# Attention values on 64x64 array tiles, and a slot that opens with scores, then the probabilities' transposition, then projections

## The reference, cut to what matters

```python
def attn_layer(x, Wqkv, qs, ksc, Wo):
    q, k, v = jnp.split(x @ Wqkv, 3, -1)            # then split into 16 heads of 64
    q = l2norm(q) * qs
    k = l2norm(k) * ksc
    q = q * cos * scale + rotate_half(q) * sin * scale
    k = k * cos * inv + rotate_half(k) * sin * inv
    out = local_attention(q, k, v)
    return out @ Wo
...
def local_attention(q, k, v):                        # keys: the window before and the own one
    sim = jnp.einsum('bhwie,bhwje->bhwij', bq, bk2) * QK_SCALE
    sim = jnp.where(mask, -jnp.finfo(sim.dtype).max, sim)
    attn = jax.nn.softmax(sim, -1)
    out = jnp.einsum('bhwij,bhwje->bhwie', attn, bv2)
...
for i in range(DEPTH):
    x = attn_layer(shift_tokens(x), ...) + x
    x = ffn_layer(shift_tokens(x), ...) + x
```

## Time and profile before

| | us |
|---|---|
| median of 3 runs | 1662.98 |
| lowest, highest | 1661.52, 1663.18 |
| the profiled execution's own time | 1662.44 |
| its span, first to last instruction | 1660.6 |
| PE busy in it | 1581.1 |
| DVE busy | 1471.4 |
| ACT busy | 1430.6 |
| POOL busy | 1313.8 |

### The profile page before, as it was taken

One profiled execution on the slowest core, in us unless ns is written; L12 is line 12 of the kernel. 1 busy time (PEld: TensorE's weight loads), 2 busy tenths in 40 slices (PEclk: granted clock), 3 DMA queues, 4 the chain that ended last, 5 costly groups with the idle time before them and its releaser, 6 DMA issues.

```text
span 1660.6 us, 68799 instructions
## 1 busy us (share of the span) xinstructions
PE 1581.1 (95%) x25860; PEld 1210.2 (73%) x25860; DVE 1471.4 (89%) x3011; ACT 1430.6 (86%) x2851; POOL 1313.8 (79%) x1305
## 2 busy tenths in 40 slices
PE   7879999999999999999999999999999999999995
PEld 5657777777777777777777777777777777777773
DVE  4499999999999999999999999999999999999874
ACT  4267998998999899899889989989998999999985
POOL 6188888888888888888888888888888888778855
PEclk9799999999999999999999999999999999999997
DMA  4111111111111111111111111111111101110100
GB/s 138 51 39 40 41 34 38 32 46 37 46 38 32 38 38 43 44 40 33 32 38 44 46 42 32 33 32 51 40 43 38 32 28 41 40 33 27 32 22 26
DMA packets 41425, 66.39 MB, mean 40 GB/s; under 512 B 7072, under 2 KB 16032, under 8 KB 41376
## 3 DMA queue, kind: packets, MB, share of 16 engines
q1 hardware_dynamic: 40224, 65.38, 13.2%
q10 hardware_dynamic: 1152, 0.34, 0.1%
HBM read 20.61 MB, written 1.05 MB: 13 GB/s over the span
## 4 chain that ended last, share of the span: by engine, by line
PE 58%; DVE 26%; issue 12%; ACT 2%; DVEq 1%; DMA 0%; POOL 0%; ACTq 0%; POOLq 0%
PE ps_s L539 13%; PE ps_a L539 11%; PE ps_qk L539 10%; PE ps_f L539 8%; PE ps_po L539 7%; DVE qk_rot L1269 5%; PE ps_v L539 5%; DVE qk L1267 4%; PE ps_po L658 4%; DVE ssq L1275 4%; DVE row_sum L1311 3%; DVE row_max L1302 3%; DVE prob L1305 2%; PE ps_f L747 1%; DVE xc L1324 1%
## 5 line engine op out<-in xcount | busy, mean ns | idle before, releaser
L436 POOL TENSOR_TENSOR qk<-qk,rnorm 128x512 f32<-128x512 f32 x384 | 393.0, 1044 | 132.1 <-DVE rnorm L1295 123.3
L428 POOL TENSOR_TENSOR qk<-qk,qk_rot 128x512 f32<-128x512 f32 x384 | 484.4, 1283 | 0.0
L443 POOL TENSOR_TENSOR prob<-prob,row_inv 128x512 f32<-128x512 f32 x192 | 200.4, 1044 | 115.5 <-DVE row_inv L1314 115.5
L1275 DVE TENSOR_REDUCE ssq<-squares 128x8 f32<-128x512 f32 x384 | 260.4, 678 | 3.4 <-ACT squares L959 3.4
L1267 DVE TENSOR_TENSOR qk<-ps_qk,table 128x512 f32<-128x512 f32 x384 | 262.2, 683 | 1.1
L1269 DVE TENSOR_TENSOR qk_rot<-ps_qk,table 128x512 f32<-128x512 f32 x384 | 260.7, 679 | 0.0
L959 ACT ACTIVATE squares<-ps_qk 128x512 f32<-128x512 f32 x384 | 232.1, 604 | 11.5 <-PE ps_qk L539 3.8
L953 ACT COPY p_bd<-ps_po 64x512 f32<-64x512 f32 x378 | 217.1, 574 | 21.0 <-PE ps_po L658 18.7
L539 PEld LDWEIGHTS ps_s<-ident,qk 128*128 128x128 f32 x1528 | 170.9, 140 | 77.6 <-DVE prob L1305 64.1
L539 PE MATMUL ps_s<-ident,qk 128*128 128x128 f32 x1528 | 202.9, 276 | 23.8 <-DVE prob L1305 22.9
L539 PE MATMUL ps_qk<-w_hi,xs_hi 128*128 (+1 forms) x384 | 188.7, 491 | 12.9 <-DVE qk_rot L1269 6.8
(11 more groups left out here) (207 smaller groups left out, 3490.4 us busy)
## 6 DMA issues: line engine op xcount, KB each, us to landing
v_back<-v_own SPq DMA_DIRECT2D x192, 192.0 KB, 2.4
w_raw<-in_wqkv SPq DMA_DIRECT2D x48, 192.0 KB, 2.4
v_back<-v_own SPq DMA_DIRECT2D x96, 64.0 KB, 2.1
wo_sb<-in_wo SPq DMA_DIRECT2D x12, 256.0 KB, 3.0
w_sb<-in_w SPq DMA_DIRECT2D x6, 341.0 KB, 3.0
w_sb<-in_w SPq DMA_DIRECT2D x6, 192.0 KB, 2.5
x_in<-in_x SPq DMA_DIRECT2D x4, 256.0 KB, 4.7
out<-s_out SPq DMA_DIRECT2D x8, 128.0 KB, 1.9
```

The costliest lines, as they stand in the source:

```text
L428: nc.gpsimd.tensor_tensor(qk[:, s, i, :], qk[:, s, i, :], qk_rot[:, s, i, :], ALU.add).then_inc(added, 1)
L436: nc.gpsimd.tensor_tensor(heads(qk[:, s, i, :]), heads(qk[:, s, i, :]), rnorm[:, s, 8 * i:8 * i + 8].unsqueeze(2).to_broadcast([P, 8, HEAD ...
L443: nc.gpsimd.tensor_tensor(heads(prob[:, s, :]), heads(prob[:, s, :]), row_inv[:, s, :].unsqueeze(2).to_broadcast([P, 8, HEAD]), ALU.mult). ...
L1275: V.tensor_reduce(ssq[:, s, 8 * i:8 * i + 8], heads(squares[:, s, OCTET * i:OCTET * i + OCTET]), AX, ALU.add).then_inc(ssq_done, 1)
```

## The change

`values` gets tiles of 64 rows by 64 columns. The key positions' two halves (`later` = 0, 1; each is one window) are multiplied apart, each with its own 32 columns of probabilities, and the two row tiles write to two banks. So `p_bd` with its zeros becomes `p_t`, a plain copy of the transposition; `keep_p` is one copy of 128 rows where it was two of 64, and the memset of `p_bd` goes. The 16 matmuls of a unit become 32, which move 32 columns where they moved 64.

The two banks are `ps_po` and `ps_q`, of each the first 256 columns; four banks are now one tensor, `ps_vpqk`, whose name the order of the changed kernel shows for `ps_v`, `ps_po`, `ps_q` and `ps_k`. Since `values` writes to `ps_q`, it waits for `q_scaled` of unit u (`pe.wait_ge(q_scaled, u + 5)`, with its own u being four less), and the next q projection waits for `attn_copied`. The q projection moves behind `scores` and `turn_p`. No other engine's order is changed but for `keep_p`.

```diff
@@ values
-            def values(u, n, j, s, ps=ps_po):
+            def values(u, n, j, s):
+
+                pe.wait_ge(q_scaled, u + 5)
+                values_into(valued, u, n, j, s)
+
+            def values_into(area, u, n, j, s):
 
                 pe.wait_ge(p_turned, u + 1)
                 pe.wait_ge(v_shifted[j], (n + 1) * (32 if j % 2 else 16))
+                nc.tensor.sem_inc(pe_passed, 1)
                 for c in range(PAIRS):
                     for odd in range(2):
+                        v = v_own if odd else v_back
                         for head in range(2):
-                            v = v_own if odd else v_back
-                            o = ps[64 * head:64 * head + 64, P * c:P * c + P].rearrange(
-                                "p (h o q) -> p h o q", h=2, o=2)[:, :, odd, :]
-                            last = mm(o, v[:, j, 64 * (2 * c + head):64 * (2 * c + head) + 64],
-                                      p_bd[:, s, 8 * head + 4 * (c // 2) + 2 * odd + c % 2].rearrange("p a b -> p (a b)"), True, True,
-                                      skip_group_check=True)
+                            for later in range(2):
+                                rows = slice(64 * later, 64 * later + 64)
+                                to = 64 * c + WINDOW * odd
+                                at = P * (2 * head + c // 2) + 64 * odd + WINDOW * (c % 2)
+                                last = mm(area[64 * head:64 * head + 64, later, to:to + WINDOW],
+                                          v[rows, j, 64 * (2 * c + head):64 * (2 * c + head) + 64],
+                                          p_t[rows, s, at:at + WINDOW], True, True, skip_group_check=True)
@@ body of TensorE
-                    project(n, j, 0, ps_q, q_scaled, q_done)
                     if live(u - 3):
                         scores(u - 3, (j - 3) % UNITS, (j - 3) % 2)
                     if live(u - 4):
                         turn_p(u - 4, j % 2)
+                    if live(u - 5):
+                        wait(pe, attn_copied, u - 4)
+                    project(n, j, 0, ps_q, q_scaled, q_done)
                     project(n, j, 1, ps_k, k_scaled, k_done)
@@ ScalarE
-                for h in range(2):
-                    rows = slice(64 * h, 64 * h + 64)
-                    last = copy(p_bd[rows, s, :, h, :], ps[rows, :].rearrange("p (g q) -> p g q", q=WINDOW))
-                last.then_inc(p_turned, 1)
+                copy(p_t[:, s, :], ps[:]).then_inc(p_turned, 1)
...
-                copy(attn_t[:, PAIRS * octet:PAIRS * octet + PAIRS, 1 + P * tile:1 + P * tile + P],
-                     ps[:].rearrange("p (c t) -> p c t", t=P)).then_inc(attn_copied, 1)
+                copy(attn_t[:, PAIRS * octet:PAIRS * octet + PAIRS, 1 + P * tile:1 + P * tile + P].rearrange(
+                    "p c (g t) -> p g c t", g=2), area.rearrange("p g (c t) -> p g c t", t=64)).then_inc(attn_copied, 1)
```

More of the change, by code:

```diff
@@ L70, in bank, with banks @@
             return ctx.enter_context(nc.psum_tensor(name, [P, 512], F32))
-        def bank_pair(name):
-            return ctx.enter_context(nc.psum_tensor(name, [P, 2, 512], F32))
+        def banks(name, n):
+            return ctx.enter_context(nc.psum_tensor(name, [P, n, 512], F32))
         def sem(name):
@@ L112, in build @@
         prob = sb("prob", [P, 2, OCTET])
-        p_bd = sb("p_bd", [P, 2, PAIRS * 4, 2, WINDOW])
+        p_t = sb("p_t", [P, 2, OCTET])
         row_max = sb("row_max", [P, 2, 8])
@@ L149, in build @@
         w1_early = [staged[l % 2][:, 2 * FF * (l // 2):2 * FF * (l // 2 + 1)] for l in range(DEPTH)]
-        ps_qk, ps_s = bank_pair("ps_qk"), bank_pair("ps_s")
-        ps_q, ps_k, ps_qs, ps_tk = ps_qk[:, 0, :], ps_qk[:, 1, :], ps_s[:, 0, :], ps_s[:, 1, :]
-        ps_v, ps_po, ps_a, ps_f = (bank(n) for n in ("ps_v", "ps_po", "ps_a", "ps_f"))
+        ps_vpqk, ps_s = banks("ps_vpqk", 4), banks("ps_s", 2)
+        ps_v, ps_po, ps_q, ps_k = (ps_vpqk[:, i, :] for i in range(4))
+        ps_vp, ps_pq, ps_qk = (ps_vpqk[:, i:i + 2, :] for i in range(3))
+        ps_qs, ps_tk = (ps_s[:, i, :] for i in range(2))
+        ps_a, ps_f = (bank(n) for n in ("ps_a", "ps_f"))
         def scored(pair):
             return pair[:, :, 0:OCTET // 2]
+        valued = scored(ps_pq)
         x_loaded = [sem(f"x_loaded_{p}") for p in range(TWOS)]
@@ L381, in _ @@
         def _(pool):
-            nc.gpsimd.memset(p_bd[:], 0.0)
             nc.gpsimd.memset(k_t[:, :, :, 0:WINDOW], 0.0)
@@ L650, in turn_into, with turn_p @@
                 last.then_inc(done, 1)
-            def turn_p(u, s, ps=ps_po):
-                if ps is ps_po:
+            def turn_p(u, s, ps=ps_po, turning=True):
+                if turning:
                     wait(pe, attn_copied, u)
@@ L835, in drain @@
                 pe.wait_ge(q_scaled, END)
+                pe.wait_ge(attn_copied, a)
                 turn_into(ps_q, c, 0, 0)
@@ L844, in drain @@
                 scores(c, 2, 0, ps_qk, False)
-                values(a, LAST, 0, 0)
+                pe.wait_ge(v_copied, END)
+                values_into(scored(ps_vp), a, LAST, 0, 0)
                 ln_spread(LAST - 2, END, STEPS + BATCHES - 4)
-                pe.wait_ge(v_copied, END)
-                turn_p(b, 1, ps_v)
                 ln_mean(LAST - 1)
                 scores(d, 3, 1, ps_s, False)
+                pe.wait_ge(attn_copied, a + 1)
+                turn_p(b, 1, ps_v, False)
                 ff_up(LAST - 2, 0)
-                pe.wait_ge(attn_copied, a + 1)
-                values(b, LAST, 1, 1)
+                values_into(scored(ps_vp), b, LAST, 1, 1)
                 ln_variance(LAST - 1)
                 ff_up(LAST - 2, 1)
-                turn_p(c, 0, ps_v)
+                pe.wait_ge(attn_copied, b + 1)
+                turn_p(c, 0, ps_v, False)
                 ff_up(LAST - 2, 2)
                 pe.wait_ge(sub_done, c + 1)
-                values(c, LAST, 2, 0, ps_k)
+                values_into(scored(ps_qk), c, LAST, 2, 0)
                 out_projection(LAST, 0)
-                turn_p(d, 1, ps_v)
+                turn_p(d, 1, ps_v, False)
                 ln_spread(LAST - 1, END + 1)
                 pe.wait_ge(sub_done, END)
+                pe.wait_ge(attn_copied, c + 1)
                 up_into(ps_q, LAST - 1, 0)
@@ L866, in drain @@
                 up_into(ps_f, LAST - 1, 2)
-                values(d, LAST, 3, 1)
-                down_into(ps_v, LAST - 3)
+                values_into(scored(ps_vp), d, LAST, 3, 1)
+                down_into(ps_k, LAST - 3)
                 out_projection(LAST, 1)
-                down_into(ps_k, LAST - 2)
+                down_into(ps_v, LAST - 2)
                 ln_mean(LAST)
@@ L1005, in start_norms, with keep_attention @@
                 nc.scalar.activation(rn_0[:, s, :], ssq_ln[:, s, :], ACT.Exp, scale=-0.5).then_inc(rn_started, 1)
-            def keep_attention(u, m, j, ps=ps_po):
+            def keep_attention(u, m, j, area=valued):
                 octet, tile = j // 2, j % 2
@@ L1107, in drain @@
                 keep_turned_k(d, 3, ps_tk)
-                keep_attention(a, LAST, 0)
+                keep_attention(a, LAST, 0, scored(ps_vp))
                 softmax_exp(c, 0)
@@ L1113, in drain @@
                 softmax_exp(d, 1)
-                keep_attention(b, LAST, 1)
+                keep_attention(b, LAST, 1, scored(ps_vp))
                 up_from(ps_f, LAST - 2, 1, ff_pairs[1])
@@ L1120, in drain @@
                 keep_p(d, 1, ps_v)
-                keep_attention(c, LAST, 2, ps_k)
+                keep_attention(c, LAST, 2, scored(ps_qk))
                 up_from(ps_f, LAST - 2, 2, ff_pairs[1])
                 gelu_spare(LAST - 2, ff_pairs[1][1])
-                keep_attention(d, LAST, 3)
+                keep_attention(d, LAST, 3, scored(ps_vp))
                 up_from(ps_q, LAST - 1, 0, ff_pairs[2])
@@ L1423, in drain @@
                 silu_invert(2)
-                after_ff(LAST - 3, ps_v)
+                after_ff(LAST - 3, ps_k)
                 after_attention(LAST)
                 ln_center(LAST)
-                after_ff(LAST - 2, ps_k)
+                after_ff(LAST - 2, ps_v)
                 ln_var(LAST)
```

## The result

| | before | after |
|---|---|---|
| median of 4 runs each, us | 1663.08 | 1754.88 |
| lowest to highest | 1661.52 to 1672.42 | 1752.22 to 1760.06 |
| span of the profiled execution | 1660.6 | 1752.9 |

The changed kernel is slower by a ratio of 1.0554, with a 95% interval of 1.0525 to 1.0584: 92 us. The forecast was 1722, so 59 of the 92 us were foreseen. The time lies inside the stated range.

The account below looks back on a forecast made before the run. TensorE and VectorE were taken to bound the kernel by turns; slots of 8.09, 7.98, 8.51 and 8.89 us make 33.47 a step, +1.24 times 48 = 60 us, giving 1722 us, range 1685 to 1775.

Parts of the forecast that it names:

- Values' price: Values on TensorE, 64x64 tiles: price unchanged at 1.08 us, as each matmul still loads 64 columns.
- The rival of cheaper values: Values on TensorE run at the scores' pace and cost 0.29 us less (0.79): 1694 us, chance 0.14.
- the loads in turn: Row tiles take turns at loading weights on TensorE, so values take 1.87 us: 1836 us, chance 0.07.
- The chain of slot 1: From scores' start: ScalarE's squares at 2.17 us, `rn` done 4.55; VectorE's `newton` at 4.58, q's rotation done 6.98.
- The rival of a covered `newton`: VectorE runs at least 2.1 us behind TensorE entering slot 1, no new wait: 1600, more likely 1615 us, chance 0.08.
- The new wait: Values on TensorE wait for VectorE's rotation of q: 1.28 us in slot 1, and again in slot 2.
- I take nothing for it: ScalarE's `keep_p` as one copy saves 0.57 us in each slot, but was given no worth in the time.
- The sum: Slots 1, 2, 3, 0 together 33.47 us a step against 32.23: +1.24, times 48 = 60 us.
- The 0.05 that I took for a change of tile size: Slots 3 and 0: values no longer share the output projection's tile size, 0.05 us lost in each.
- the 0.11 of before: Change of tile size ahead of scores, 0.11 us: goes in slots 1 to 3, kept behind `ln_spread` in slot 0.

Follow-up runs that it names:

- The order alone: The kernel before with only TensorE's order changed (scores, transposition of the probabilities, then q projection), values and their bank as before: 1777.49 us.
- the values alone: The changed kernel with the q projection first in TensorE's slot again, so it waits at once for the copy of attention: 1823.85 us.
- the wait last: The changed kernel with values' wait for the rotation of q last of their three waits in place of first: 1740.52 us, ratio 1.0457.

## Why the prediction was right, and what it missed

**Values' price** stood: 1.06 against 1.08, set by the 64 loaded columns, as the run with twice the moved columns shows. The rival of cheaper values is refuted (no records at the scores' pace), and so are the loads in turn (0.12 for two rounds of four tiles, not 0.24). The Trainium skill (TensorEngine Tiling (Array Packing), "Theoretical Speedup") speaks of up to twice the speed with a contraction of 64 or less; the trace shows none of it here, 1.06 where twice the speed would be 0.54. On the same page the Trainium skill ("Key Properties") says that tiles load and multiply side by side; there the trace agrees, at 0.058 us a load on four tiles at once.

**The chain of slot 1** stood to 0.02 us at each of its links, and the run with the norms ahead of the squares shows that it causes the loss. The rival of a covered `newton` fell: VectorE idled 2.20 us ahead of it.

**The new wait** of values is where the lateness enters TensorE in the changed kernel, as said. But the argument made it look needed. The order alone loses 114 us without it, through ScalarE's queue and the mask. The prediction named VectorE's queue behind `newton` and left out ScalarE's behind `rn`.

**"I take nothing for it"**, the step on `keep_p`, was wrong as a statement of worth: it is worth 42 us here. It did no harm to the sum only because that sum followed VectorE's and TensorE's path alone, which with the single copy is the longest. With two copies the same sum would have been another 42 us short.

**The sum**, 1.24 us a step against 1.91 measured in the loop, is the term that was mis-sized. Its parts, by slot:

| | predicted | after | what was missing |
|---|---|---|---|
| slot 1 | 8.09 | 8.31 | a late start of values costs 0.25, not 0.03 |
| slot 2 | 7.98 | 7.89, mean 8.04 | half clock in 22 steps |
| slot 3 | 8.51 | 8.62 | idle time at the loop's turn |
| slot 0 | 8.89 | 9.02 | the price of two changes of tile size |
| step | 33.47 | 33.84, mean 34.01 | |

For slot 0 the rows are these; the output projection took 1.84 until values (1.74 before), and `ln_spread` 0.37 until scores (0.19 before, where a q projection followed):

```profile
852.52 1.91 PE L542 MATMUL ps_a<-attn_t,wo_sb 128*64 128x257 f32 x16
854.36 0.32 PE L542 MATMUL ps_vpqk<-p_t,v_back 64*64 64x32 f32 x8
...
855.42 0.43 PE L758 MATMUL ps_f<-ident,rnorm 128*128 128x128 f32 x2
855.79 0.63 PE L542 MATMUL ps_s<-k_t,q_t 64*32 64x64 f32 x40
```

The 0.05 that I took for a change of tile size was 0.10. Behind `ln_spread` I had kept the 0.11 of before; the row is 0.18 longer now. At the loop's turn, scores with their three waits now stand where the q projection stood, and TensorE idles 0.25 where it idled 0.15:

```profile
846.78 0.85 PE L542 MATMUL ps_s<-k_t,q_t 64*32 64x64 f32 x64 [0.25 <-issue]
```

So the shown step is 0.37 us longer than forecast. Another 0.30 lies between the shown steps and the means: the step of before is 0.13 longer than its mean (32.23 against 32.10), and that of the changed kernel is one without half clock and 0.17 shorter than its mean. The half clock, 22 times 0.40 us, is 0.21 a step; against it, the last steps of the loop are shorter in both kernels.

Outside the loop the sum was off as well. Slot 1 of step 5 begins at 243.6 us after and at 228.7 before, 15 us later where 5.25 steps at 1.24 make 6.5; TensorE's mean clock up to there is 0.88 against 0.93. How much of the 15 us is the clock and how much the thinner work of those steps was not taken apart. The drain, which the prediction left as it was, became shorter: from the start of its first scores to the end it takes 56.0 us where it took 61.2; no run was made for that.

## What to carry to other kernels

When an instruction is moved later in one engine's list, follow everything that stands behind its first reader in that reader's queue: here a table load and two small operations behind the squares of q cost 82 us, and their order on ScalarE cost nothing to change. Before splitting matmuls onto more tiles, compare the time to load the stationary columns with the time to move the others; if the load is the longer, halving the moved ones gives little or nothing, as here. A table load or another long fixed cost belongs ahead of an instruction that has to wait, not behind it.

## What the runs showed of the hardware

- **A short wait went with a lower clock.** The changed kernel, with TensorE idle 1.53 us (as the profile counts it) ahead of values in slot 1, ran 3.4 us at the 1.2 GHz level in two of three steps past 489 us. With 1.43 us of idle, or with the same wait pattern and busier values, the loop ran at 2.4 GHz throughout. The difference was worth some 10 us. Two other runs have such stretches in their loops: the order alone 16, with an idle time of 1.90 us in each step ahead of the scores of slot 2, and keep_p in two halves 8, with 1.53 us. The sum of idle time alone does not decide it: the values alone idle 3.70 us a step, the changed kernel 2.16, and yet their loop has no such stretch; their longest single idle time is 1.23 us. What exactly decides stays open; no run was made for it.
- **The loads set the pace on 64x64 tiles too.** Float32 loads of 64 columns follow each other on a tile every 0.058 us, on four tiles at once; 32 or 64 moved columns make 1.06 or 1.09 us of a unit's values. The tiles of two row groups do load side by side.
- **A wait instruction behind the late one costs time on TensorE.** With one more behind it, the matmul starts 0.25 us after the rotation's end (slot 1 of the changed kernel), with none behind it 0.15 (its slot 2, and both slots with the wait last).
- **A change of tile size** between an output projection (128x64 tiles) and values (64x64) costs 0.10 us (1.84 against 1.74 for the output projection of slot 0).
